# One semaphore per parity for a tile's middle layer, and no waits for blocks already seen

## The reference

```python
# mixture 0: 8 experts, 2 picks per token, hidden 512
h = relu(xf @ W1e + b1e)            # 128 -> 512
y = h @ W2e + b2e                   # 512 -> 128
acc = acc + cwe[:, None] * y        # over the experts, weights of the 2 picks
# mixture 1: 8 groups of 8 experts, 2 x 2 picks per token, hidden 256
h = relu(einsum('td,gedh->tgeh', xt, W1) + b1)
y = einsum('tgeh,gehd->tged', h, W2) + b2
out = sum over groups and experts of y * c2 * c1
```

## Time and profile before

| | |
|---|---|
| median of 3 runs | 1138.37 us |
| runs | 1137.57 to 1139.75 us |
| span of the profiled execution | 1221.9 us |
| mean granted TensorE clock in it | 0.767 of 2.4 GHz |
| instructions | 18019 |
| TensorE matmul busy | 66% of the span |
| VectorE busy | 64% |
| GpSimd busy | 42% |

### The profile page before, as it was taken

The page is one execution under the profiler, slowest core; times in us unless marked ns, Lnnn a source line. Parts: engine busy times, 40 slices in busy tenths (PEclk is TensorE's granted clock), DMA queues, the critical chain, the costliest instruction groups (busy, mean ns, idle before and its releaser), DMA issues.

```text
span 1221.9 us, 18019 instructions
## 1 busy us (share of the span) xinstructions
PE 802.4 (66%) x5133; PEld 637.8 (52%) x5133; DVE 778.2 (64%) x2305; ACT 437.9 (36%) x1233; POOL 510.6 (42%) x528
## 2 busy tenths in 40 slices
PE   0218963879998248778587511287887897888343
PEld 0105552679998124434255401177776787777332
DVE  7885467656665248888766699855555555666642
ACT  2543241524444134443103304533343444444200
POOL 7841001255540634662101002466664435555574
PEclk9759965579999556666665555599999998999755
DMA  2290089012221287566400404133332223333222
GB/s 69 76 403 37 1 249 309 1 50 70 71 66 38 60 143 140 118 143 131 77 1 1 132 0 127 33 85 85 89 83 81 83 77 87 88 96 94 59 72 75
DMA packets 116599, 112.95 MB, mean 92 GB/s; under 512 B 16403, under 2 KB 102994, under 8 KB 116258
## 3 DMA queue, kind: packets, MB, share of 16 engines
q1 hardware_dynamic: 103228, 84.68, 25.3%
q0 software_dynamic: 13280, 27.13, 8.2%
HBM read 76.15 MB, written 35.57 MB: 91 GB/s over the span
## 4 chain that ended last, share of the span: by engine, by line
PE 55%; DVE 22%; issue 9%; POOL 5%; ACT 4%; DMA 3%; another core or an unknown queue 1%; SPq 0%; DVEq 0%; POOLq 0%; ACTq 0%
PE ps L638 18%; PE ps L645 15%; DVE wide L1348 6%; PE ps L1969 4%; POOL wide L810 3%; PE ps L633 3%; DVE wide L1229 3%; PE ps L2231 3%; PE ps L2139 2%; PE ps L2180 2%; ACT wide L1757 2%; DVE bnst L955 2%; POOL wide L874 1%; PE ps L2076 1%; PE ps L2224 1%
## 5 line engine op out<-in xcount | busy, mean ns | idle before, releaser
L645 PE MATMUL ps<-big,wide 128*128 x1568 | 238.1, 282 | 33.9 <-ACT wide L605 20.6
L638 PE MATMUL ps<-wide 128*128 (+1 forms) x1580 | 247.1, 287 | 18.9 <-DVE wide L554 12.2
L867 POOL DMA_INDIRECT wide<-xrows,holder x189 | 182.8, 967 | 158.1 <-PE ps L633 116.1
L559 DVE TENSOR_SCALAR wide<-ps,wide 128x128 f32<-128x128 f32 x395 | 131.7, 348 | 156.9 <-PE ps L638 138.4
L638 PEld LDWEIGHTS ps<-wide 128*128 128x128 f32 x1580 | 206.2, 195 | 40.8 <-issue 32.9
L645 PEld LDWEIGHTS ps<-big,wide 128*128 128x128 f32 x1568 | 203.7, 194 | 44.5 <-issue 43.9
L605 ACT ACTIVATE wide<-ps,wide 128x128 f32<-128x128 f32 x395 | 137.8, 367 | 202.4 <-PE ps L638 184.9
L1348 DVE TENSOR_REDUCE wide<-ps 125x3 f32<-125x1500 f32 (+1 forms) x96 | 143.7, 1540 | 46.7 <-PE ps L1969 45.3
L874 POOL DMA_INDIRECT wide<-results,place x128 | 127.6, 997 | 100.1 <-DVE h L1328 44.0
L1969 PE MATMUL ps<-big 97*125 97x500 bf16 x256 | 104.8, 545 | 40.3 <-DVE wide L1348 32.5
L623 ACT COPY wide<-ps 128x128 f32<-128x128 f32 x322 | 85.2, 264 | 92.1 <-PE ps L645 78.1
(11 more groups left out here) (388 smaller groups left out, 1102.7 us busy)
## 6 DMA issues: line engine op xcount, KB each, us to landing
results<-wide SPq DMA_DIRECT2D x161, 128.0 KB, 1.8
big<-kappa SPq DMA_DIRECT2D x8, 1750.0 KB, 21.0
big<-parts SPq DMA_DIRECT2D x96, 125.0 KB
big<-in_L_ffn_W_dram SPq DMA_DIRECT2D x10, 1024.0 KB, 9.4
big<-in_L_ffn_W_dram SPq DMA_DIRECT2D x64, 128.0 KB, 2.6
parts<-wide SPq DMA_DIRECT2D x24, 250.0 KB
xrows<-wide SPq DMA_DIRECT2D x2, 1792.0 KB
wide<-results,place POOLq DMA_INDIRECT x192
```

What stands on the lines that cost most here:

```text
L559: last = v.tensor_scalar(ring.hid[u % 2][:, 128 * k:128 * k + 128], ps[:, 4 + u % 2, 128 * k:128 * k + 128], w[:, hid + k:hid + k + 1], 0. ...
L638: last = t.matmul(ps[:, (2 if k < c.HC // 2 else 4) + u % 2, 128 * k:128 * k + 128], ring.w1[u % U][:, 128 * k:128 * k + 128], turned, sta ...
L645: last = t.matmul(ps[:, 6 + u % 2, 0:D], ring.hid[u % 2][:, 128 * k:128 * k + 128], w[:, D * k:D * k + D], start=k == 0, stop=k == c.HC - 1)
L867: gp.indirect_dma_start(ring.rows[j % RING], None, xrows[:, :], bass.IndirectOffsetOnAxis(ap=holder[:, j:j + 1], axis=0)).then_inc(S(f"row ...
```

## The change

VectorE and ScalarE both raise one semaphore, `hid0` for even tiles and `hid1` for odd ones, by one each when their half of a tile's middle layer is done. TensorE waits once, for the count that both halves of this tile and of all earlier ones of its parity make: 2 * (tile // 2) + 2. The start values of 2 that the old semaphores were given go away. TensorE also remembers, while the program is written, the highest count of `blocks_in` that it has waited for, and writes no wait for a lower or equal one. The waits at the end of a mixture go to the two new semaphores.

```diff
+        def middles(tile):
+            return 2 * (tile // 2) + 2
...
-            sp.wait_ge(S(p + "hid_dve"), c.tiles + 3)
-            sp.wait_ge(S(p + "hid_act"), c.tiles + 3)
+            for u in range(2):
+                sp.wait_ge(S(p + f"hid{u}"), middles(c.tiles - (c.tiles - u) % 2))
...
-                last.then_inc(S(p + "hid_dve"), 1)
+                last.then_inc(S(p + f"hid{u % 2}"), 1)
...
-            dve.sem_inc(S(p + "hid_dve"), 2)
...
-                last.then_inc(S(p + "hid_act"), 1)
-            act.sem_inc(S(p + "hid_act"), 2)
+                last.then_inc(S(p + f"hid{u % 2}"), 1)
...
+            seen = 1
...
                         pe.wait_ge(S(f"row_ld{n % RING}"), 16 * (n // RING) + 16 + earlier_rows(c, n))
-                        pe.wait_ge(S(p + "blocks_in"), n - 1)
+                        if n - 1 > seen:
+                            seen = n - 1
+                            pe.wait_ge(S(p + "blocks_in"), seen)
                         turn(n)
-                    if first_tile + u + 1 < c.tiles:
-                        pe.wait_ge(S(p + "blocks_in"), c.blocks_for(first_tile + u + 1))
+                    if first_tile + u + 1 < c.tiles and c.blocks_for(first_tile + u + 1) > seen:
+                        seen = c.blocks_for(first_tile + u + 1)
+                        pe.wait_ge(S(p + "blocks_in"), seen)
                     pe.wait_ge(S(p + "w1_ready"), first_tile + (u + 4))
                     first(u + 1, words.value(u, 1))
-                    pe.wait_ge(S(p + "hid_dve"), first_tile + (u + 3))
-                    pe.wait_ge(S(p + "hid_act"), first_tile + (u + 3))
+                    pe.wait_ge(S(p + f"hid{u % 2}"), middles(first_tile + u))
                     second(words.value(u, 0), u)
```

More of the change, by code:

```diff
@@ L660, in expert_tensor @@
                 pe.wait_ge(S("w1_late"), 16 * (c.E - W2_EARLY))
+            seen = 1
             def tiles(first_tile, count):
+                nonlocal seen
                 for u in range(count):
@@ L2267, in _ @@
                 pe.wait_ge(S(q + "res_ready"), c.tiles + 2)
-                pe.wait_ge(S(q + "hid_dve"), c.tiles + 3)
-                pe.wait_ge(S(q + "hid_act"), c.tiles + 3)
+                for u in range(2):
+                    pe.wait_ge(S(q + f"hid{u}"), middles(c.tiles - (c.tiles - u) % 2))
                 if f == 0:
```

## The result

The changed kernel took 1125.1 us, median of 4 runs (1122.1 to 1128.2), beside 1138.1 us (1137.57 to 1139.75) for the kernel before: 0.9894 of its time, 95% interval 0.9869 to 0.9919. The forecast was 1124.0 us.

The account below looks back on a forecast made before the run. TensorE was taken as the bound: its array in mixture 0, its sequencer in mixture 1's odd tiles. Gains of 6.4 and 11.0 us, less 17%, made 14.4 us: 1138.4 - 14.4 = 1124.0 us; own range 1117 to 1130, 8-in-10 range 1111 to 1138.

Parts of the forecast that it names:

- Which waits are instructions: In TensorE's tile loops, 640 of 18019 instructions go; in mixture 1, 45 transpose waits and 80 on `w1_ready` stay.
- Mixture 0 at nothing: Mixture 0's 70 tiles lose 138 instructions without gain, beside an always busy array; without that cover, 13.8 us.
- Hidden: Rival: TensorE's sequencer runs ahead of the array, so the instructions cost nothing; gain 0 to 2 us, about 1137.5; chance 0.14.
- The price of 0.10 us: Each removed wait instruction on TensorE's sequencer in mixture 1 is worth 0.10 us, between bounds of 0.051 and 0.12.
- the ring of two tiles: Mixture 1's repeating path through ScalarE's middle layer and TensorE's sequencer: 2.11 us falls to 1.91, above the array's 1.78.
- Cheap waits: Rival: each removed instruction is worth only its recorded 51 ns; 7.4 us gained, 1131.0 us; chance 0.18.
- From ScalarE's end to the load of `second`, 0.14 us: In mixture 1, the time from ScalarE's end to TensorE's weight load of `second` falls from 0.24 to 0.14 us.
- The sum of tiles 78 to 251: Mixture 1: 0.10 us a tile, 6.4 us in tiles 78 to 141 and 11.0 us in 142 to 251.
- Tiles 0 to 77 at nothing: Mixture 1's first part gains nothing counted, since each tile needs a gather of 1.24 us; other end 7.8 us.
- All of it: Rival: tiles 0 to 77 gain as well and a wait is worth 0.12 us; 25 us gained, 1113 us; chance 0.10.
- The pauses and the 17%: Mixture 1's late ScalarE starts leave VectorE leading, so 17% is taken off: 17.4 x 0.83 = 14.4 us.
- Slower: gathers that close up: Rival: mixture 1's gathers lose their rests and cost 0.81 us each instead of 0.25; 1168 us; chance 0.08.

Follow-up runs that it names:

- number 10: Changed kernel with two fulfilled waits on `w1_ready` ahead of the middle-layer wait in every tile of mixture 0: 1127.51 us (0.9908).
- number 2: Half of the change: one count per parity, all waits for blocks kept; 1130.25 us, 0.9938 of the kernel before.
- number 3: Half of the change: waits for blocks already seen left out, both middle-layer counts kept; 1128.66 us, 0.9929 of the kernel before.
- number 1: The kernel before, unedited, traced a second time ("the kernel before again"): 1137.8 us against 1137.14 (1.0005), span 1137.1 us.
- number 4: Changed kernel with a fulfilled `w1_ready` wait in every tile of mixture 1, written behind the middle-layer wait, run ahead of the arrival: 1126.99 us (0.9906).
- number 6: Changed kernel with TensorE's table load moved behind `first` of the next even tile, ahead of the middle-layer wait: 1116.65 us (0.9824).
- number 9: Changed kernel with TensorE's table load moved, and gathers with additions in two of four tiles instead of three: 1135.6 us (0.9984).
- number 11: Changed kernel with VectorE's table load moved one tile later, to the next even tile: 1127.68 us (0.9915).
- number 7: Kernel before, all waits kept, with TensorE's table load moved behind `first` of the next even tile: 1118.01 us (0.9837).
- number 8: Kernel before with TensorE's table load moved, and gathers with additions in two of four tiles instead of three: 1142.86 us (1.0054).
- number 5: Changed kernel with a fulfilled `w1_ready` wait in every tile of mixture 1, written ahead of the middle-layer wait: 1129.34 us (0.9938).

## Why the prediction was right, and which of its steps were not

**Which waits are instructions.** Right. 643 records went (18019 to 17376) where 640 were counted; 45 and 80 stay, and none at the single wait. The rival that the change doesn't do what it says is out.

**Mixture 0 at nothing.** Right, and shown from both sides: the change took 138 instructions away and number 10 put 70 back, with 129.8 us each time. The Trainium skill's "TensorE: Matmul & The Clock Gate", section "Architectural detail: the array is 16× 32×32, not 1× 128×128", gives TensorE a queue 64 deep. That such a queue hides the sequencer's work was my conclusion from it and not what the section says. In mixture 0 the conclusion fits; in mixture 1 it does not, for there the same kind of instruction moved the loop by 11.9 us. *Hidden* is out, since the ratio's interval ends at 0.9919.

**The price of 0.10 us.** Right for the instruction. Numbers 2 and 3 took one each out of the ring of two tiles and their quickest tenth fell from 2.12 to 2.02 and 2.01; the two together gave 1.92 in a typical quick pair. *Cheap waits*, at 0.051 us, is out as a mechanism, and its 1131.0 us lie above the interval's end (0.9919, 1128.9 us).

**From ScalarE's end to the load of `second`, 0.14 us.** Wrong. It is 0.21 (947.16 to 947.37): the load now lies close behind the one before it, which began 0.44 us earlier, so here the array and not the sequencer is last. The ring is nevertheless shorter by the full 0.20 us, for the sequencer, once through its register operation, has its table load behind it sooner (in the mean 0.314 us after ScalarE's end, where it was 0.405): what counts is 0.80 us to the next `first` and not where `second` begins. I had put the 0.10 us at the wrong stretch of the right ring.

**The sum of tiles 78 to 251.** This is the term that was mis-sized. It was 6.4 us for tiles 78 to 141 and 11.0 for 142 to 251, before the deduction, and measured 3.6 and 6.9: 10.5 us where 17.4 stood. The table load, which I had carried at 0.33 us through the change, is a piece of the same ring and grew while the ring tightened: from 0.33 to 0.38 us in the mean of the last stretch's 43 pairs and from 0.33 to 0.41 in the 34 pairs of tiles 79 to 146. That is 43 x 0.052 + 34 x 0.077 = 4.8 of the 6.9 us that are missing. Another 0.7 us are missing at the end: from tile 240 to tile 251 the kernel before took 10.6 us and the changed one 10.2, where 1.1 was to be gained. No table load is due for the last eight tiles, and they ran near the array's pace in both kernels. Order of time at the loop's end, the kernel before again and then the changed one:

```profile
1059.52 0.53 PEld L638 LDWEIGHTS ps<-wide 128*128 128x128 f32 x4
...
1061.33 0.53 PEld L638 LDWEIGHTS ps<-wide 128*128 128x128 f32 x4
```

```profile
1049.68 0.53 PEld L639 LDWEIGHTS ps<-wide 128*128 128x128 f32 x4
...
1051.47 0.53 PEld L639 LDWEIGHTS ps<-wide 128*128 128x128 f32 x4
```

Two tiles take 1.81 and 1.79 us. The remaining 1.4 us are small delays between the ring's pieces (the pairs with a short load, too, lie 0.03 us above 1.92 in the mean), and what causes them isn't known. Nor is it known why the load grew.

**Tiles 0 to 77 at nothing.** Right, as far as the traces can tell. The 1.4 us between the two traces are no more than one kernel differs from the next: the traces with the change's waits have 91.7 to 93.0 us for this stretch (numbers 4, 6, 9, 10, 11 and the change), those with the waits of before 92.4 to 93.1 (numbers 1, 7, 8). The gathers held that stretch, one every 1.25 us in the changed kernel as well; order of time, GpSimd:

```profile
826.03 0.94 POOL L872 DMA_INDIRECT wide<-xrows,holder  x1 [0.30 <-issue]
827.28 0.94 POOL L872 DMA_INDIRECT wide<-xrows,holder  x1 [0.30 <-issue]
```

A tile takes 1.18 to 1.19 us here in every trace but the first, less than a gather's 1.25, since TensorE starts with a lead and uses part of it: in the changed kernel 10 gathers have started before tile 0 and 83 before tile 77, 73 in 90.6 us. *All of it* is out.

**The pauses and the 17%.** Wrong in its ground. I multiplied by 0.83 for a loss that ordinary executions don't have; of the 68 us that mixture 1 lost in the first trace none is in the second (278.6 us, and I had worked out 278 for a loop without them). The span after, forecast at 1207.5 us, was 1126.4. That the time nevertheless came to 1125.1 where 1124.0 was forecast is in part luck. Without the deduction my sum would have been 1138.4 - 17.4 = 1121.0 us, 4.1 too low. The 3.0 us taken off for pauses that aren't there hid part of the 6.9 us that I had put too high; the two errors have nothing to do with each other. The time itself fell by 13.0 us by the medians, where the two traces show 11.9 in the loop and could place 10.5 in the tiles that I had counted.

***Slower: gathers that close up.*** Not seen. In number 6 gathers stand back to back, 1.25 us from start to start, closer than the change brings them, and the last stretch is quicker (0.940 us a tile) than in the changed kernel, where rests remain between them (0.985). The changed kernel's tiles 147 to 251 took 102.6 us after 109.2, so the sign that I had named didn't come. The price of 0.81 us a gather had been read from a stretch of the execution with the pauses.

## What to carry to other kernels

Find the ring that sets a loop's pace and follow it through the sequencer too; a wait whose record shows 51 ns cost up to 0.10 us a turn of the ring here (0.07 in the mean) when it stood behind the arrival that the engine waits for, and nothing when it stood ahead of it or beside a full array. So before removing waits, look at what is queued behind the arrival and could stand before it: moving one table load gave 19 us, where removing 640 waits gave 13, and the two together no more than the first alone. And where a trace's span is far from the timed runs, trace the same kernel again before pricing anything from it.

## What the runs showed of the hardware that was not expected

- One execution of the kernel before had a span of 1221.9 us where a second one of the same program had 1137.1; 68 us of the difference lay in mixture 1, where ScalarE started up to a microsecond after the matmuls that it waited for the earlier trace rows. What caused it isn't known.
- The table load on TensorE's sequencer has no fixed length. In the last stretch it took 0.33 to 0.34 us in the mean in the kernels that have one or both of the removed instructions behind the arrival (numbers 1, 2, 3, 5, 7, 8), and 0.38 to 0.41, with single ones up to 0.54, where neither is there (the change, numbers 4, 6, 9, 10, 11). But those instructions are not what keeps it short: in the first trace of the kernel before, which has both, it took 0.38 us in the mean there and up to 0.61, and in tiles 79 to 146 of number 2 it took 0.37. Number 11 and the second trace of before exclude VectorE's load as the cause; the cause is open.
- Of two waits in a row the one written last became the instruction of its own (numbers 4, 5, 10), and two equal waits in a row became one (number 10).
